# Two PSUM banks by turns for the scores and the small stages, two-part q, k and v, and a second gather tile in a macaron block

## The reference, cut to what matters

```python
x = x + 0.5 * ffn(layernorm(x))      # "first"
x = x + attn(layernorm(x))
x = x + 0.5 * ffn(layernorm(x))      # "second"
# ffn: 2 experts of 1024 hidden units, top-1 routing by gate_w:
#   y = (silu(x @ w_gate.T) * (x @ w_up.T)) @ w_down.T * prob_of_chosen
# attn: xn = rms_norm(x) * rms_w; q, k, v = xn @ Wq, Wk, Wv; 16 heads of 16
#   scores = q @ k.T / 16, causal, softmax, @ v, @ Wo, + x
```

## Time and profile before

| | us |
|---|---|
| median of 3 runs | 1332.26 |
| lowest, highest | 1330.32, 1336.48 |
| the profiled execution | 1319.46 |
| its span, first to last instruction | 1317.7 |
| TensorE busy | 1096.0 (83%) |
| VectorE busy | 960.4 (73%) |
| ScalarE busy | 711.8 (54%) |
| GpSimd busy | 527.7 (40%) |

### The profile page before, as it was taken

One profiled execution on the slowest core, in us unless ns is written; L12 is line 12 of the kernel. 1 busy time (PEld: TensorE's weight loads), 2 busy tenths in 40 slices (PEclk: granted clock), 3 DMA queues, 4 the chain that ended last, 5 costly groups with the idle time before them and its releaser, 6 DMA issues. The chain is left out here.

```text
span 1317.7 us, 39560 instructions
## 1 busy us (share of the span) xinstructions
PE 1096.0 (83%) x14564; PEld 946.3 (72%) x14564; DVE 960.4 (73%) x2040; ACT 711.8 (54%) x1331; POOL 527.7 (40%) x663
## 2 busy tenths in 40 slices
PE   0787789968999888888788898997979989788895
PEld 0766667757778776777676687876867878677784
DVE  6545547796888878878878887888878888675431
ACT  4434315655566565655655665675646655555321
POOL 3154443254523344443334533334543253343432
PEclk9898889998999899999899899998999999889998
DMA  9120352213221124123222141112422112311111
GB/s 319 58 81 26 105 93 60 86 54 86 74 83 48 34 70 114 39 66 91 69 75 74 54 126 51 39 57 67 100 74 61 52 51 72 82 47 42 50 45 45
DMA packets 115665, 96.16 MB, mean 73 GB/s; under 512 B 52288, under 2 KB 109376, under 8 KB 115488
## 3 DMA queue, kind: packets, MB, share of 16 engines
q1 hardware_dynamic: 98400, 66.88, 18.3%
q0 software_dynamic: 6144, 16.79, 4.3%
q10 hardware_dynamic: 10944, 9.97, 2.4%
HBM read 45.75 MB, written 37.88 MB: 63 GB/s over the span
## 5 line engine op out<-in xcount | busy, mean ns | idle before, releaser
L620 POOL TENSOR_TENSOR h_lo<-hid,h_hi 128x256 bf16<-128x256 f32 x304 | 221.2, 748 | 515.3 <-ACT h_hi L684 514.9
L760 ACT ACTIVATE area<-ps_st 128x512 f32<-128x512 f32 x320 | 190.5, 595 | 288.2 <-PE ps_st L1166 285.2
L953 DVE TENSOR_REDUCE row_min<-ps_s 128x1 f32<-128x512 f32 (+2 forms) x384 | 183.5, 505 | 79.2 <-PE ps_s L1145 78.0
L1077 PE MATMUL ps_g<-x_t,w 128*128 128x128 f16 x1104 | 211.5, 226 | 16.0 <-issue 8.8
L1079 PE MATMUL ps_u<-x_t,w 128*128 128x128 f16 x1104 | 211.5, 225 | 0.0
L1079 PE MATMUL ps_g<-x_t,w 128*128 128x128 f16 x1104 | 211.3, 226 | 0.0
L1077 PE MATMUL ps_u<-x_t,w 128*128 128x128 f16 x1104 | 211.1, 225 | 0.0
L1078 PE MATMUL ps_g<-x_t,w 128*128 128x128 f16 x1104 | 210.6, 225 | 0.0
L1078 PE MATMUL ps_u<-x_t,w 128*128 128x128 f16 x1104 | 209.9, 223 | 0.0
L971 DVE TENSOR_TENSOR area<-area 128x512 f16<-128x512 f32 x256 | 199.3, 779 | 9.7 <-ACT area L761 9.6
L1143 PE MATMUL ps_s<-kt,qt 96*128 96x512 bf16 (+3 forms) x512 | 139.6, 311 | 73.1 <-DVE row_min L953 56.8
(11 more groups left out here) (162 smaller groups left out, 2847.1 us busy)
## 6 DMA issues: line engine op xcount, KB each, us to landing
qk_scratch<-area SPq DMA_DIRECT2D x32, 384.0 KB, 2.6
qt<-qk_scratch SPq DMA_DIRECT2D x192, 64.0 KB, 2.7
kt<-qk_scratch SPq DMA_DIRECT2D x192, 64.0 KB, 2.7
y_sorted<-ys ACTq DMA_DIRECT2D x76, 128.0 KB, 1.7
x_buf<-x SPq DMA_DIRECT2D x8, 512.0 KB, 4.8
out<-x_buf SPq DMA_DIRECT2D x8, 512.0 KB, 2.9
x_sorted<-yt SPq DMA_DIRECT2D x18, 128.0 KB, 1.9
area<-w_down SPq DMA_DIRECT2D x4, 512.0 KB, 13.7
```

Of the source, the lines that this page charges most:

```text
L620: pool.tensor_tensor(h_lo[:, u % 2, c], hid[:, u % 2, c], h_hi[:, u % 2, c], ALU.subtract).then_inc(h_lo_done, 1)
L760: act.activation(p_f32[:, f % 3], ps_st[:], ACT.Exp, scale=-1.0)
L953: ins = dve.tensor_reduce(row_min[:, p % 2, h + hh, i:i + 1], ps_s[:, at:at + P * (i + 1)], AX.X, ALU.min)
L1077: pe.matmul(cols, w_hi, x_hi, start=kb == 0 and f == 0, stop=False, skip_group_check=True)
```

## The change

1. `scores` and all small stages share two banks, `ps_w0` and `ps_w1`, by turns in the order of the list. Each waits for the release of the stage two turns back. `SPARE` units use the two `ps_v` banks, and the last slot of pass 1 is among them.
2. q, k and v have two fp16 parts, with weights scaled by a power of two (a third `w_scale` stage). The ScalarE copy and the VectorE subtraction of a third part are gone. The scores matmul has 64 rows, and one of zeros; the transposed one has 68. `pv` has 33 columns. 8 DMAs bring a part's q and k in, not 12. `ones` fills a row of q as well, at unit 8 rather than 19.
3. In the fills of block 2, minima are taken over four pieces of 128 columns in one operation; one small operation for a part joins them.
4. There are two `yt` tiles. `x_update` stands 3 points later, but for a "first" batch not later than one point before its norm.

```diff
-QPART = [0, 1, 2, 0, 1, 0]
-KPART = [0, 0, 0, 1, 1, 2]
+QPART = [0, 1, 0, 1]
+KPART = [0, 0, 1, 1]
-VW = 3 * HD + 1
+MAX_ROWS = 3
+MAX_AT_ROW = ROWS + 1
+VW = 2 * HD + 1
-ONES_UNIT = 19
+ONES_UNIT = 8
-         if q == 1 and n in (0, 1, len(PASSES) - 1) and (n, s) != (1, SLOTS[1] - 1)]
+SPARE = [u for u, (n, s, q) in enumerate(UNITS) if q == 1 and n in (0, 1, len(PASSES) - 1)]
-S_FILLS = [[(0, 3, 0)], [(1, 3, 0)], [(0, 2, 0), (0, 0, 384)], [(1, 2, 0), (1, 0, 384)], [(0, 1, 0), (1, 1, 256)]]
+S_FILLS = [[(0, 3, 0)], [(1, 3, 0)], [(0, 0, 0), (0, 2, 128)], [(1, 0, 0), (1, 2, 128)], [(0, 1, 0), (1, 1, 256)]]
-REST_LAG = 1.7
+STORE_LAG = 1.0
+GATHER_LAG = 8
+UPDATE_LAG = 16
-SCALE_AT = [-50.5, 3.9]
+SCALE_AT = [-50.5, 3.9, 23]
-        put(end + 13, "x_update", k)
+        at = end + UPDATE_LAG
+        if what == "first":
+            at = min(at, part_at(GROUPS * b, NORM_AT[0]) - 1)
+        put(at, "x_update", k)
...
-            if st[0] in ("transpose", "proj", "out_proj", "row_max", "l_prefix", "w_scale"):
-                free[st] = last
-                last = {"transpose": lambda b, kind, kb: (xt_lo_done, 2 * sets[b, kind] + kb + 1),
-                        "proj": lambda b, m: (rest_done, NP * b + m + 1),
+            if st[0] in ("transpose", "proj", "out_proj", "row_max", "l_prefix", "w_scale", "scores"):
+                n = len(free)
+                bank_of[st], free[st] = ps_w[n % 2], turns[n % 2]
+                turns[n % 2] = {"transpose": lambda b, kind, kb: (xt_lo_done, 2 * sets[b, kind] + kb + 1),
+                                "proj": lambda b, m: (part2_done, NP * b + m + 1),
...
+                                "scores": lambda p, f: (max_done, FILLS * p + f + 1)}[st[0]](*st[1:])
...
-                    if n:
-                        pool.wait_ge(x_updated, n)
+                    if n >= 2:
+                        pool.wait_ge(x_updated, n - 1)
...
-                    pool.memset(kt[ROWS:ROWS + 3].bitcast(F32), TWO_ONES).then_inc(ones_ready, 1)
+                    pool.memset(qt[ROWS:ROWS + 1].bitcast(F32), 0.0)
+                    pool.memset(kt[ROWS:ROWS + 1 + MAX_ROWS].bitcast(F32), TWO_SCALES).then_inc(ones_ready, 1)
...
+                    elif k == 2:
+                        dve.scalar_tensor_tensor(out=rms_abs[:], in0=rms_col[:], scalar=-1.0, in1=rms_col[:],
+                                                 op0=ALU.mult, op1=ALU.max)
+                        for kb in range(KB):
+                            w = GU_PIECES + DOWN_PIECES + kb
+                            dve.wait_ge(w_in[w], 16)
+                            ins = dve.tensor_reduce(wa_max[:, kb:kb + 1], stage[w][:, 0:WO], AX.X, ALU.max,
+                                                    apply_absolute_value=True)
...
-                        ins = dve.tensor_tensor(
-                            v_parts[b % 2][:, 2 * g:2 * g + 2, :, 2 * HD:3 * HD],
-                            rest[:, m % 2, :].rearrange("p (i h d) -> p i h d", i=2, h=H),
-                            v_parts[b % 2][:, 2 * g:2 * g + 2, :, HD:2 * HD], ALU.subtract)
...
-                        ins = dve.tensor_tensor(qk_parts[:, c, 2, :], rest[:, m % 2, :],
-                                                qk_parts[:, c, 1, :], ALU.subtract)
...
-                        for hh, i, at in S_FILLS[f % KINDS]:
-                            ins = dve.tensor_reduce(row_min[:, p % 2, h + hh, i:i + 1], ps_s[:, at:at + P * (i + 1)],
-                                                    AX.X, ALU.min)
+                        ins = dve.tensor_reduce(minima[:, kind - 2, :, 0], ps[:].rearrange("p (j n) -> p j n", j=T),
+                                                AX.X, ALU.min)
                     ins.then_inc(max_done, 1)
+                    if f == FILLS - 1:
+                        dve.wait_ge(max_done, FILLS * p + f)
+                        dve.tensor_reduce(row_min[:, p % 2, :, 0, 2], row_min[:, p % 2, :, 1:, 0], AX.X,
+                                          ALU.min).then_inc(min_done, 1)
...
-                    dve.tensor_reduce(o_sum[:], ps_o[pair % 2][:, :, :, 0:3 * HD].rearrange("p h i (r d) -> p h i d r", r=3),
+                    dve.tensor_reduce(o_sum[:], ps_o[pair % 2][:, :, :, 0:2 * HD].rearrange("p h i (r d) -> p h i d r", r=2),
...
-                    if FILLS * p + f:
-                        pe.wait_ge(max_done, FILLS * p + f)
-                    else:
-                        pe.wait_ge(gated, LAST_EARLY + 1)
```

More of the change, by code:

```diff
@@ L244, in macaron @@
         ys = [sb(f"ys{n}", [P, D], F32) for n in range(2)]
-        yt = sb("yt", [P, T, D], F32)
+        yt = [sb(f"yt{n}", [P, T, D], F32) for n in range(2)]
         xt_hi = sb("xt_hi", [P, KB, S], F32R)
@@ L252, in macaron @@
         h_lo = sb("h_lo", [P, 2, S], BF16)
[L254 to L259, removed]
+        qt = sb("qt", [P, H, S], F16)
+        kt = sb("kt", [P, H, S], F16)
+        v_parts = [sb(f"v_parts{n}", [P, T, H, VW], F16) for n in range(2)]
+        area = sb("area", [P, 11 * S], F32)
         xn = area[:, 0:T * D].rearrange("p (i d) -> p i d", i=T)
[L261 to L264, removed]
+        qk_parts = area[:, 2 * S:4 * S].bitcast(F16).rearrange("p (c r n) -> p c r n", c=2, r=2)
+        p_f32 = area[:, 4 * S:7 * S].rearrange("p (r n) -> p r n", r=3)
+        p_f16 = area[:, 7 * S:11 * S].bitcast(F16).rearrange("p (k r n) -> p k r n", k=2, r=4)
         p_hi, p_lo = p_f16[:, 0], p_f16[:, 1]
@@ L489, in _ @@
                     sp.dma_start(batch_view(out, b), x_of(b)[:]).then_inc(x_out[b], 16)
-                elif what == "proj_rest" and PROJ[st[2]][0] != "v":
+                elif what == "qk_store" and PROJ[st[2]][0] != "v":
                     b, m = st[1:]
@@ L669, in _ @@
                     act.activation(e_abs[:], neg_abs[:], ACT.Exp, scale=1.0 / XSCALE).then_inc(l_exp, 1)
-                elif what == "gate" and st[2] == KB - 1:
+                elif what == "tanh":
                     u = st[1]
@@ L695, in _ @@
                     if s == 0 and n >= 2:
-                        act.wait_ge(gathered, 64 * ITEM_AT[n - 1])
+                        for parity in range(min(ITEM_AT[n - 1], 2)):
+                            act.wait_ge(gathered[parity], 64 * ((ITEM_AT[n - 1] + 1 - parity) // 2))
                     act.dma_start(y_sorted[n % 2][s * P:(s + 1) * P, :], ys[g % 2][:]).then_inc(y_saved[g % 2], 16)
@@ L715, in _ @@
                     scale = rms_col[:, kb:kb + 1] if kind == "attn" else 1.0
-                    act.activation(xt_hi[:, kb, :], ps_m[:], ACT.Copy, scale=scale).then_inc(xt_hi_done, 1)
+                    act.activation(xt_hi[:, kb, :], ps[:], ACT.Copy, scale=scale).then_inc(xt_hi_done, 1)
                 elif what == "proj":
@@ L874, in _ @@
                     ins.then_inc(x_updated, 1)
-                elif what == "up" and st[2] == KB - 1:
+                elif what == "hid":
                     u = st[1]
@@ L945, in _ @@
+                    ins.then_inc(part2_done, 1)
+                elif what == "row_min":
                     p, f = st[1:]
+                    ps = bank_of["scores", p, f]
                     dve.wait_ge(s_done, FILLS * p + f + 1)
-                    h = 2 * (f // KINDS)
-                    if f % KINDS == KINDS - 1:
-                        ins = dve.tensor_reduce(row_min[:, p % 2, h:h + 2, 1], ps_s[:].rearrange("p (h n) -> p h n", h=2),
+                    kind, h = f % KINDS, 2 * (f // KINDS)
+                    minima = row_min[:, p % 2, h:h + 2]
+                    if kind == KINDS - 1:
+                        ins = dve.tensor_reduce(minima[:, :, 0, 1], ps[:].rearrange("p (h n) -> p h n", h=2),
@@ L1024, in _ @@
             for st in order:
-                what = st[0]
+                what, ps = st[0], bank_of.get(st)
                 if free.get(st):
@@ L1045, in _ @@
                     for m in range(T):
-                        ins = pe.matmul(ps_m[:, m + 1:T + 1], ones[:], sel0[i][:, 0:T - m], start=False,
+                        ins = pe.matmul(ps[:, m + 1:T + 1], ones[:], sel0[i][:, 0:T - m], start=False,
                                         stop=m == T - 1, skip_group_check=True)
```

249 lines of the change are left out of this document (131 added, 118 removed).

## The result

The changed kernel took 1297.52 us (median of 4 runs, 1295.1 to 1303.01), against 1333.54 us for the kernel before (4 runs, 1330.32 to 1336.48). The ratio is 0.9736, with a 95% interval of 0.9696 to 0.9776: 36 us less. The forecast was 1266 us, 66 less; the time lies within the range and the direction is as forecast, but nearly half of the gain is missing.

The account below looks back on a forecast made before the run. PE, 83% busy and working through a fixed-order list, was taken as the bound, with its waits and half clock. Terms 54 + 12 + 2 + 6 + 14 - 4 - 3 - 15 = 66 us took 1332 to 1266 us; range 1230 to 1310.

Parts of the forecast that it names:

- Two banks, and the small stages: Scores fills stop waiting for the previous minima: 54 us (25 to 64); small stages for a projection's rest: 12 (0 to 13.4).
- for all this I give back 15 us: PE reaches transposed scores and pv sooner and waits there, DVE's queue stays as deep: 15 us lost (0 to 50).
- The gather: Second gather tile and later update remove most of DVE's mid-kernel gather waits; no separate gain, PE's share already in scores' waits.
- The clock: Of PE's 11 waits of 2.5 us or more, 7 go, at 2 us each: 14 us gained (0 to 22).
- the clock stays low: Rival, chance 0.06: fewer long but more short PE waits, no 14 us, 0.01 less middle clock, 10 us more: 1290 us.
- 6 us were counted for 47: DVE works 47 us less, making minima, low parts and hidden values earlier; worth 6 us to PE (0 to 14.8).
- pv: PE's pv matmuls with 33 columns gain nothing at full clock; 2 us for half-clock stretches (0 to 21).
- The start: Third scale stage in PE's path costs 4 us (2 to 7); earlier row fills on POOL cost 3 (0 to 7).
- DVE as the bound: Rival, chance 0.20: PE's waits only move to low parts and hidden values; only 30 of DVE's 47 us count: 1302 us.
- too much coupled: Rival, chance 0.07: small stages among scores make turns wait, 64 waits of 1.5 us; slower, 1347 us.
- all goes: Rival, chance 0.12: nothing given back, clock recovers fully, pv gives half its upper bound, scores their last 8: 1227 us.
- little: Rival, chance 0.05: other waits take up all but a few us; time within 7 us of 1332.

Follow-up runs that it names:

- the two runs: Against the changed kernel: one extra unused 128x512 VectorE subtraction per projection, 1271.41 us (0.963); block 2's minima again in two operations without the joining one, 1268.14 us (0.9602).
- the update at 13 points: Changed kernel with both tiles of gathered outputs kept but x_update back at its old place (13 points, not 16), on a pausing chip: 1291.4 us, 0.9702.

## Why the prediction was right, and where it was too large

**Before and after were of two sorts of chip.** The prediction took a profiled time of 1319.46 us, added the 12.8 us to the median of 1332.26 and kept them. The 12.8 us are no distance from profiled to timed runs: the median of the kernel before is 1319.6 on a quiet chip, its lowest time on a pausing one 1324.96, and its profile has no "remote". So the profile is of a quiet chip and the timed runs are not. In like terms the forecast is 1319.5 - 66 = 1253 for a quiet chip, and 1263.15 was measured. That error is 10 us. The other 20 to 22 (34 that the changed kernel loses on a pausing chip, less the 12 to 14 that the kernel before loses) were in no step. That the forecast still lies in its range owes something to the range's width, since the range was not drawn for this. A pause in the profile after (start, us, instruction, idle before):

```profile
343.88 0.22 PE L1118 MATMUL ps_g<-x_t,w 128*128 128x128 f16 x1
...
345.25 0.22 PE L1119 MATMUL ps_g<-x_t,w 128*128 128x128 f16 x1 [1.15 <-issue]
...
345.51 0.69 ACT L785 ACTIVATE area<-ps_st,s_scale 128x512 f32<-128x512 f32 x1 [1.11 <-remote]
```

PE stands 1.15 us in the middle of a row of matmuls that wait for nothing, and ACT meanwhile too; DVE executes one operation in it. In the profile after, PE has 33 us of "issue" idle in 40 places, and 23 to 25 us in the other three profiles of a pausing chip; in all ten profiles of quiet chips, the kernel before among them, it is 9 to 10 us in 2 to 4 places. The releaser "remote" sums to 72 to 99 us in the four, and to nothing in the ten. What stops the engines isn't named by any row. Nor are the pauses all of it. The span of the changed kernel is 37.0 us longer in the profile of the first timing than on a quiet chip: PE's "issue" idle makes 24 of it, and PE is busy for 16.9 us longer. Most of that is the clock: busy time times the missing share of the clock, summed over steps of 1 us, is 60 us there and 48 on the quiet chip, 12 us more. Why the changed kernel loses more than the kernel before stays open, as there is no profile of the kernel before on a pausing chip.

**The sum as a whole.** The two profiles of quiet chips can be set against the sum. PE's idle time fell from 221.7 to 177.1 us, by 44.6, where the terms for waits give 54 + 12 + 6 - 15 - 4 - 3 = 50. Its busy time fell from 1096.0 to 1087.2, by 8.8, where the clock and pv were to give 14 + 2 = 16, and of the 8.8 only 1 to 2 are half clock (below). The profiled execution after is the slowest of its five, 3 us above their median. So on a quiet chip the waits were priced nearly right in sum, and the term that failed is the clock.

**Two banks, and the small stages.** The mechanism is shown. Put in alone the turns bring 24 us, and taken out they cost 26 to 28, where the step had 54 + 12 us. The waits themselves were sized well: those of fills for minima went from 72.9 to 12.4 us (54 less was forecast), and of the 13.4 us in which small stages waited for a projection's rest 2.6 stay. What was too small is "for all this I give back 15 us". The fill doesn't ask for its minima any more, but the next stage with a late product does: with the banks alone 31 us stand in other rows beside the 48 gone, and in the changed kernel 8.4 us are new as prefix sums (L1081) that wait for minima, and the waits for exponentials grew from 14.8 to 25.1 us where the sum let 6 go. In the sum the gather's own term makes up for it.

**The gather.** The step sized the waits rightly (50.0 to 17.8, of which 12.4 at the end), and put nothing on it, as "in the first sum already". It is a term of its own, 22 to 23 us, about half of it waits and half clock. It read a point as 1.25 us; 1000 us for 32 x 21 points are 1.5. By medians, turns and gather taken out are 28 + 23 = 51 us, where the sum had 54 + 12 + 14 - 15 = 65.

**The clock.** 14 us were counted for 7 long waits that go. The price of one was about right (the stretches at half clock lose 1.5 to 3.1 us of busy time each), but the count was not. The ten longest waits of the fills did go (none over 1.4 us is left), but waits for exponentials, low parts and others of the same length came in their place: between 200 and 1200 us PE had 14 waits of 2.4 us or more, of all kinds (the prediction has 11), and has 11. One of them, for exponentials, and the 12 us around it, where the clock is 0.72 as it was before around the wait of 4.48 us for minima:

```profile
722.99 0.50 PE L1198 MATMUL ps_st<-qt,kt 68*128 68x384 f16 x1 [4.69 <-ACT area L786]
...
716.00:728.00 12.00, 6.97 (x71) 5.70 (x69) 8.97 (x29) 5.74 (x11) 7.30 (x11) 0.72 0.19 62
```

Read in steps of 1 us, the granted clock goes to 0.5 in 18 stretches of the middle before and in 16 after, and the busy time lost by it over the whole span is 50 us before and 48 after. The mean granted clock is 0.949 on the quiet chip, against 0.950 before, and 0.96 over the middle stretch in both the earlier trace rows. The rival "the clock stays low" was right in its first half, no 14 us, and wrong in its second, since 0.01 of clock wasn't lost either. The Trainium skill's section on depth-cycling (TensorE: Matmul & The Clock Gate) tells of a kernel that lost by banks in rotation; here the rows show no such loss.

**DVE.** Its operations cost what they were sized at. The forms of the changed kernel on a quiet chip:

```profile
L987 DVE TENSOR_REDUCE row_min<-ps_w 128x4 f32<-128x512 f32 x128 | 88.0, 688 | 38.6 <-PE ps_w L1181 38.4
L1020 DVE TENSOR_REDUCE o_sum<-ps_v 128x128 f32<-128x256 f32 x64 | 26.6, 416 | 8.6 <-PE ps_v L1218 8.6
L966 DVE TENSOR_TENSOR v_parts<-ps_w,v_parts 128x512 f16<-128x512 f32 x16 | 11.1, 693 | 14.1 <-ACT v_parts L760 14.1
L992 DVE TENSOR_REDUCE row_min<-row_min 128x4 f32<-128x12 f32 x32 | 5.3, 165 | 0.0
```

688 for the 683 forecast, 416 for 415; 693 for 780, as strips cost nothing here; 165 ns for the upper bound of 279. In all DVE is busy for 43.3 us less (960.4 to 917.1), where 47 were forecast. What was too small is the worth: 6 us were counted for 47. At the 0.2 to 0.3 us for each that the two runs give (the second up to 0.4, uncertain), 47 us are 10 to 14 us by estimate. The rival had 30.

**The missed cost.** Nothing in the prediction speaks of the scale column. It could have been read: in the trace before, the same line with and without a column is 83 ns apart.

```profile
L716 ACT ACTIVATE xt_hi<-ps_m,rms_col 128x512 fp32r<-128x512 f32 x16 | 10.9, 680 | 3.9 <-PE ps_m L1111 3.9
...
L716 ACT ACTIVATE xt_hi<-ps_m 128x512 fp32r<-128x512 f32 x16 | 9.6, 597 | 20.1 <-PE ps_m L1111 20.1
```

640 x 0.083 = 53 us of ACT would have been the estimate; 57 came, which cost 4 to 6 us. The Trainium skill (ScalarE: Activation LUTs, "What ACT_TABLE_LOAD costs") gives about 93 ns for each operand that is a per-partition pointer; the runs agree, with 91 and 88.

**pv.** Right: 33 columns are no faster than 49.

```profile
902.46 0.35 PE L1218 MATMUL ps_v<-v_parts,area 128*128 128x33 f16 x8
902.66 0.32 PE L1198 MATMUL ps_st<-qt,kt 68*128 68x384 f16 x1
```

Eight in 0.20 us at full clock, 25 ns each, as before.

**The start.** 7 us were given, and 8.2 are seen: the first update moves from 109.89 to 118.09 us. The new scale stage is in PE's list with 2.28 and 1.46 us of waiting, 3.7 for the 4 of the step (profile of the first timing; the two waits are the same on the quiet chip):

```profile
63.19 0.27 PE L1071 MATMUL ps_w<-ident,w_max 128*1 128x128 f32 x1 [2.28 <-DVE w_max L819]
64.92 0.17 PE L1073 MATMUL ps_w<-w_two,ones 1*128 1x2 bf16 x1 [1.46 <-DVE w_two L828]
```

**The whole.** On quiet chips: turns 28, gather 23, DVE 10 to 14, the column -4. That is 57 to 61 by medians against 56 measured; by ratios turns and gather are 26 and 22, and it is 54 to 58. So the parts make up the whole, but what the start costs can't be read from the rest, and no run on such a chip has measured it. The parts were undone singly, so what two of them share isn't known. Of the prediction's signs of being wrong none came: fills wait 12.4 us (45), small stages for minima 8.4 (30), for exponentials 25.1 (45), and the first stretch grew by 8.2 (14). The rivals: DVE as the bound is refuted (8 us for 36.7); "too much coupled" is refuted, since small stages wait about 8 us for minima and not 96; "all goes" and "little" are outside both results. The best time is that with the constant scale, 1258.82 us, for weights like these only; of the general versions none beats the changed kernel clear of the spread (the update at 13 points comes nearest to it).

## What to carry to other kernels

A wait that falls away in a list of fixed order is not worth its length, as the same late producer is met again one stage further on. How much is left depends on what else is late: with the banks alone 48 us less of waits at the fills were worth 24 us, and with the other parts of the change in place 33 us less were worth 26 to 28. A wait of the late producer itself (DVE in front of the gather, 34 us) was worth 22 to 23 us, and half of that came by the clock. So before the clock is counted as a gain, count the long waits of every kind that stay, not only those of the sort that goes. Look through a diff for an immediate that becomes a column, and price it from any line of the trace that has both forms. And before a profiled time is set beside timed ones, see whether they can be of the same chip: the distance of 12.8 us between the two was that between the two sorts of chip, and for the changed kernel it was 34 us.

## What the runs showed of the hardware that was not expected

- Chips differ by 12 to 14 us in the kernel before and by 34 in the changed one. Four profiles from the slower ones have 31 to 40 places where ACT or DVE are released by "remote", 72 to 99 us in all, and pauses of PE of about a microsecond amid matmuls; ten from the faster ones have none.
- Of 37 us between the spans of the changed kernel on the two sorts, pauses of PE make 24 and the lower clock about 12.
- The clock fell in the same way around a wait of 4.48 us for minima and one of 4.69 us for exponentials: 0.72 over 12 us both times.
- An activation of 128x512 from PSUM takes 686 ns with its scale in a column and 595 with a constant.
- A reduction to 4 minima in rows of 128 takes 688 ns, one to a single minimum over the same 512 columns 685: the number of results costs nothing.
- DVE executed the same 1912 operations in 907.8 us on a pausing chip and in 917.1 us on a quiet one. The low parts of the exponentials (L1011, 256 operations) make 8.8 of the 9.3 us, with 763 ns against 798; the other forms shown have the same means in both. Why is not shown.
